# A new order of the side work inside the attention stages, and the second load of the input moved behind the last block of output weights

## The reference

```python
mod = (_silu(c) @ wmod).reshape(1, 6, 1, -1)             # sa, ca, ga, sb, cb, gb
h = _layernorm(x) * (1 + ca) + sa
q = _rmsnorm(h @ wq_a.T, q_ln) @ wq_b.T                  # 32 heads of 64 + 64 (rotary)
ckv, k_pe = split(h @ wkv_a.T); kv = _rmsnorm(ckv, kv_ln) @ wkv_b.T
attn = softmax(causal(q_full @ k_full.T * scale))        # per head, 1024 x 1024
x = x + ga * ((attn @ v) @ wo.T)
h = _layernorm(x) * (1 + cb) + sb
x = x + gb * (down(silu(gate(h)) * up(h)))               # integer weights, width 1376
```

## Time and profile before

| | |
|---|---|
| median of 3 runs | 720.97 us (719.98 to 726.5) |
| the profiled execution, its own time | 720.49 us |
| its span, first to last instruction | 718.7 us |
| PE, DVE, ACT, POOL busy, share of the span | 95%, 73%, 40%, 36% |
| stages 0 to 7 in the trace | 83.81 to about 483 us |
| granted TensorE clock, mean | 0.998 |

### The profile page before, as it was taken

How to read it: one execution, slowest core, us unless ns; L and a number is a source line. 1 busy time by engine, 2 the same in 40 slices (tenths; PEclk the granted TensorE clock), 3 DMA queues, 4 the chain that set the end, 5 groups by cost and what they waited for, 6 DMA issues and landing times.

```text
span 718.7 us, 9328 instructions
## 1 busy us (share of the span) xinstructions
PE 684.4 (95%) x3539; PEld 486.7 (68%) x3539; DVE 526.6 (73%) x762; ACT 288.4 (40%) x427; POOL 258.9 (36%) x164
## 2 busy tenths in 40 slices
PE   2989899999999999999999999899999999999997
PEld 1854477666676675665675665456888888887886
DVE  6878689989999999899899796796882331323432
ACT  4742344534544545445345343352444322322120
POOL 2137622934745645546538204213651000000111
PEclk9999999999999999999999999999999999999999
DMA  8935533303404304313332803810211413100101
GB/s 318 280 90 133 134 77 88 92 17 89 107 1 108 88 8 102 88 41 81 74 81 60 301 2 111 299 59 6 83 29 41 135 46 88 47 1 1 44 31 44
DMA packets 40972, 63.34 MB, mean 88 GB/s; under 512 B 5536, under 2 KB 21664, under 8 KB 39072
## 3 DMA queue, kind: packets, MB, share of 16 engines
q1 hardware_dynamic: 40928, 62.75, 32.0%
HBM read 32.99 MB, written 2.10 MB: 49 GB/s over the span
## 4 chain that ended last, share of the span: by engine, by line
PE 62%; DVE 14%; POOL 8%; DMA 8%; issue 3%; ACT 2%; SPq 2%; DVEq 0%; ACTq 0%; POOLq 0%
PE PS L975 17%; PE PS L992 8%; PE PS L798 7%; DMA Q<-TQ 5%; PE PS L861 5%; PE PS L939 5%; PE PS L868 5%; PE PS L864 5%; PE PS L879 4%; DVE MX L1423 3%; POOL RT L1738 3%; POOL RT L1737 3%; POOL TQ L1776 2%; DVE PR L1518 2%; SPq L562 2%
## 5 line engine op out<-in xcount | busy, mean ns | idle before, releaser
L1423 DVE TRANSPOSE_TENSOR_REDUCE MX<-PS 128x16 f32<-128x512 f32 x288 | 182.5, 686 | 24.3 <-PE PS L798 23.2
L1167 ACT ACTIVATE PR<-PS 128x1024 f32<-128x1024 f32 x108 | 99.5, 929 | 128.7 <-PE PS L868 90.3
L861 PE MATMUL PS<-Q,KH 96*128 96x512 f32 x288 | 118.9, 413 | 4.2 <-ACT PR L1167 2.8
L868 PE MATMUL PS<-Q,KH 97*128 97x512 f32 (+1 forms) x288 | 114.5, 397 | 0.2 <-DMA Q<-NM 0.2
L864 PE MATMUL PS<-Q,KL 96*128 96x512 f32 (+1 forms) x288 | 113.9, 395 | 0.0
L798 PE MATMUL PS<-Q,KH 96*128 96x512 f32 (+1 forms) x288 | 103.4, 422 | 3.9 <-DMA Q<-TQ 2.4
L861 PEld LDWEIGHTS PS<-Q,KH 96*128 96x128 f32 x288 | 54.8, 190 | 40.5 <-ACT PR L1167 16.9
L798 PEld LDWEIGHTS PS<-Q,KH 96*128 96x128 f32 (+1 forms) x288 | 53.0, 191 | 28.1 <-issue 13.4
L1518 DVE TENSOR_TENSOR PR<-PR 128x2048 f32<-128x2048 f32 (+1 forms) x28 | 69.3, 2476 | 0.2
L1645 DVE SCALAR_TENSOR_TENSOR wide<-PS,ffn_s,TQ 128x1024 f32<-128x1024 f32 x10 | 12.8, 1284 | 72.6 <-PE PS L975 72.6
L1167 ACT ACTIVATE wide<-PS 128x1024 f32<-128x1024 f32 (+1 forms) x48 | 45.7, 953 | 50.3 <-PE PS L868 44.2
(11 more groups left out here) (196 smaller groups left out, 1101.3 us busy)
## 6 DMA issues: line engine op xcount, KB each, us to landing
Q<-TQ SPq DMA_DIRECT2D x56, 384.0 KB, 6.5
RT<-in_wo SPq DMA_DIRECT2D x4, 1024.0 KB, 5.5
TQ<-in_wo SPq DMA_DIRECT2D x4, 1024.0 KB, 6.8
Q<-TQ SPq DMA_DIRECT2D x16, 192.0 KB, 3.4
WI<-in_gate_w SPq DMA_DIRECT2D x10, 256.0 KB, 3.3
WI<-in_up_w SPq DMA_DIRECT2D x10, 256.0 KB, 3.9
DI<-in_down_w SPq DMA_DIRECT2D x10, 256.0 KB, 2.7
PR<-in_wmod_c SPq DMA_DIRECT2D x2, 1024.0 KB, 6.3
```

What stands on the lines that cost most here:

```text
L861: pe.matmul(dst, M.KH[0:KR, ks], M.Q[0:KR, w % 2, 0, qb, :, qs], start=True, stop=False)
L868: ins = pe.matmul(dst, M.KH[0:rows, ks], M.Q[0:rows, w % 2, 1, qb, :, qs], start=False, stop=True)
L1167: act.activation(tiles, banks, ACT.Exp).then_inc(S_.p, 1)
L1423: dve.tensor_reduce(M.MX[:, kt, qt // 4, :, qt % 4, :], PS[:, bank_of(turn), :].rearrange("p (h s q) -> p h s q", h=HG, q=L), axis=AX.X, o ...
```

## The change

Two edits. The string list `STAGE` gets another order (stages 0 to 6), and in SP's program the second load of x, with the two waits ahead of it, moves from behind `load_wo(3)` to behind `load_wo(7)`. `LAST` and all functions stay.

```diff
 STAGE = [
-    "w p p", "-v8,9,10,11 p p", "p p -a10", "p", "-a11 p p", "p even0", "", "p p", "p odd0", "p p", "lat0 p low0 a1",
-    "v0,1,2,3 den1 a2 p p", "p", "p p", "p", "p p a3 p", "p", "p p split0", "p p", "p", "p p", "p inv1", "p p",
-    "v4,5 join norm1", "a5", "even1 odd1", "", "a6", "rows a7", "lat1", "", "low1 split1", "v6,7 den0 a8 inv0 norm0",
-    "", "", "a9",
+    "", "", "w p p", "-v8,9,10,11 -a10 p p", "p p", "p -a11 even0 p", "odd0", "p", "p", "p p a1", "v0,1,2,3 den1 p p",
+    "p", "inv1 a2 p p norm1", "", "p", "a3 p p p", "p", "p p", "p p", "v4,5 a5 lat0", "low0 split0 p", "p p", "p p",
+    "p", "p p", "p even1", "p join", "odd1", "a6", "lat1 rows", "", "a7 low1 split1 a8", "v6,7 den0 a9 inv0 norm0",
+    "", "", "",
 ]
@@ sp_program
     for m in range(2, G):
         load_wo(m)
-        if m == 3:
+        if m == G - 1:
             third = max((w, s) for w, s in USES if USES[w, s][0] == 2)
             sp.wait_ge(S_.pv, NSTEP * third[0] + third[1] + 1)
             sp.wait_ge(S_.ad, NADD * third[0] + ADDS.index(third[1]) + 1)
             sp.dma_start(M.x1, t["x"].rearrange("(n p) d -> p n d", p=P)).then_inc(S_.xr, 16)
```

## The result

The changed kernel takes 738.22 us in the median of its runs (732.53 to 739.0), the kernel before, measured beside it, 721.84: a ratio of 1.021, 95% interval 1.018 to 1.0245. It is slower, by 16.4 us (whether by more than 2% the interval leaves open), and the forecast was 721.4, no change. The profiled execution after took 739.0 us, with a span of 737.2.

The account below looks back on a forecast made before the run. PE, busy 95% of the span, was taken to bound the kernel, with a DVE, POOL and ACT chain holding it in the stages. 720.49 + 5.2 - 0.7 - 1.2 - 2.4 gave 721.4 us, range 715.5 to 728.

Parts of the forecast that it names:

- the chain: Stages 1 to 5: `odd1` ends on DVE 42.38 in, then 9.34 to the next stage; 51.8 each, +5.2 us in all.
- The idle time at u35: Near the stage's end PE waits for an exponential: 2.2 us of idle in each of stages 1 to 5.
- Part 10's waits: PE's waits for the queries in stages 1 to 5, about 0.38 us each with restart, were to go.
- The hidden turn: Rival, chance 0.14: DVE ends `odd1` no later than before, stages 1 to 5 stay at 50.76, total 716.2 us.
- the PE bound: Rival, chance 0.05: the next stage no longer hangs on `split1`, waits worth 6.2 us go, total 710.0.
- `a8` did not take the turn before the second sum: Forecast that DVE's addition would not precede POOL's second rotated sum; otherwise 2.28 us longer per stage, 732.8 total.
- the load: x issued behind block 7 lets block 4 of `wo` land earlier: -2.4 us (bounds 0 to -2.4).
- Fold 4: PE's fold of output weights block 4 waited 2.40 us for its transfer; that wait was to go.
- stage 0: 49.15 us against 49.82, -0.7: two more units cover the 1.11 wait for weights, and its clock fall goes too.
- stage 6: PE alone bounds it; two more units cover its wait for the queries: -1.2 us (bounds -0.8 to -1.4).
- the falling clock: Rival, chance 0.11: the clock falls behind PE's 2.2 us idle in five stages, 1.7 us each, 729.9 total.
- the 2.40 wait in stage 7: PE's wait for an output weights block; the clock stayed at 1.00 after it, cited against the clock rival.

Follow-up runs that it names:

- load-alone run: Old stage order, only the second load of x moved behind the last block of output weights, against the kernel before: 717.28 us against 720.87, ratio 0.9952.
- 11 pieces: Old stage order with the load moved, ACT's rounding of the second half in stages 0 to 5 cut into 48-column pieces: 720.24 us.
- the first experiments: The follow-up runs that start with the moved load of x alone in the old stage order: 717.28 us against 720.87 for the kernel before.
- the last kernel: The changed kernel with `odd1` put back right behind `even1`, ahead of the last part and `join`, and `rows` one place later: 710.45 us, ratio 0.985.

## Why the prediction was wrong, and what of it was right

**Right: the chain.** Without falls the kernel takes 721.69, and each step can be found in stage 4 of the kernel with eight matmuls filled in, which starts at 288.58. PE's last matmul of `even1` ends its turn at 326.12, 37.54 in (forecast 37.62). The start of the stage, of the unit behind `even1` and of the next stage on PE, then DVE:

```profile
288.58 0.50 PE L861 MATMUL PS<-Q,KH 96*128 96x512 f32 x1
...
326.12 0.39 PE L861 MATMUL PS<-Q,KH 96*128 96x512 f32 x1
...
340.31 0.50 PE L861 MATMUL PS<-Q,KH 96*128 96x512 f32 x1
```

```profile
326.32 0.69 DVE L1397 TENSOR_TENSOR RT<-PS,cos 128x512 f32<-128x512 f32 x1
...
327.53 0.70 DVE L1427 TRANSPOSE_TENSOR_REDUCE MX<-PS 128x16 f32<-128x512 f32 x1
328.27 1.59 DVE L1438 TENSOR_REDUCE NMj<-MX 128x64 f32<-128x256 f32 x2
329.78 0.67 DVE L1405 TENSOR_TENSOR RT<-PS,sin 128x512 f32<-128x512 f32 x1
...
330.97 2.27 DVE L1522 TENSOR_TENSOR PR<-PR,wide 128x2048 f32<-128x2048 f32 x1
```

`a6` starts 330.97 - 288.58 = 42.39 after the stage (forecast 42.38), and the next stage 9.34 later (9.34). That the first agrees to 0.01 is luck: PE's part came out 0.08 shorter, DVE's start 0.04 earlier, its work 0.13 longer. The idle time at u35 was 2.15 to 2.21 (2.2). Part 10's waits are gone but for one in the first maxima. The hidden turn and the PE bound are refuted with it: `odd1` on DVE follows PE's `even1` and `join`, and `split1` still holds u35. `a8` did not take the turn before the second sum.

**Right: the load.** Fold 4 waits no more, x is issued right behind block 7, and POOL's residual addition, at 514.79, does not wait for it:

```profile
484.88 0.33 SPq L601 DMA_DIRECT2D TQ<-in_wo  x1
485.32 0.39 SPq L672 DMA_DIRECT2D TQ<-in_x  x1
```

**Right, with less behind it: stage 0.** The wait for the weights went, and so did its fall. But the load-alone run waits 1.29 there and shows no fall (stage 0 takes 48.39 instead of 49.82): the 1.70 us of the earlier trace rows were one execution's chance, not a fixed part of the kernel before. Beside an execution without that fall the new order makes stage 0 longer (48.96 against 48.39), not 0.7 shorter.

**Mis-sized: stage 6.** It gained 0.65 (46.62 to 45.97) where 1.2 was reckoned, outside the bounds of 0.8 to 1.4. The wait that went was 0.80, and without it PE can't gain much more than that; and the wait of 0.41 for `join` came instead. That the total still agrees to 0.3 is partly luck: stages 0 to 5 and the load together came out 0.8 shorter than reckoned.

**Wrong: the chance of the falling clock.** The step that failed is the sentence "Against: after the 2.40 wait in stage 7 it stayed at 1.00". One wait without a fall was taken to speak for six waits of nearly the same length, in each execution. The runs show that waits of equal length at one place are followed by a fall in some turns and not in others, and that at u35 of the new order the share rises with the wait: none of 6 at 1.16, 3 of 6 at 1.59, 17 of 18 at 2.15 to 2.21. One draw at 2.40 that came out well says little against that, and stage 0's fall behind 1.11 was a row on the other side. Length alone doesn't decide: at that place in stage 0, behind another wait of 1.44 just ahead of the stage, waits of 0.88 and 1.11 were followed by a fall and waits of 0.73, 0.95 and 1.29 were not. The rival also counted five waits where there are six, since stage 0 has one too. With six in each execution and the shares measured here, some falls were all but sure; the rival belonged at the head, and the range should have held it. The Trainium skill (TensorE: Matmul & The Clock Gate, section "HAM oscillation — how this bites in real kernels") says that a loop which lets TensorE wait on every turn can pay for the slow clock on every turn; these traces agree, with falls at 17 of 18 such waits. The waits in that section's example last some 3 to 5 us; here 2.2 us were enough, and 1.59 in three cases of six.

**Wrong: its price.** The rival put 1.7 on a fall, from stage 0's 3.70 us. The short falls cost that (1.6), but three of the six in the profile after were long, 4.2 us each, and the sixth was not counted. So even the rival, at 729.9, came out 9 us short of the profiled execution.

**What stays open.** Why one wait is followed by a fall and its equal is not, and why a fall begins during the wait or only behind it, with which its length goes (3.3 us, or two or three times that). Also whether the new order is somewhat more prone at 1.6 us: with 2 matmuls filled in all six executions were above 725, with 11 pieces seven of ten lay at or below 720.33. No run had both orders with the same wait and all else equal, and these two ran on different chips.

## What to carry to other kernels

A wait of PE that a reordering makes longer, and that comes back in every turn of a loop, has two prices: its length, and a fall of the clock behind it that may or may not come. One execution's profile of a place where the clock held is little evidence that it will hold: count how many such waits the new kernel has per execution, and put the falls into the sum. Where the wait can't be removed, a few matmuls that nothing reads fill it (here four were enough and two were not); better is to look at what holds it, as here the order of `odd1` and `join` on DVE.

## What the runs showed of the hardware that was not expected

Eight matmuls without use took 16.5 us off the kernel's time, by keeping the clock at 0.999 to 1.000 (738.22 to 721.69).

The nineteen executions of the kernel before beside the first experiments fall into groups by the granted clock: 718.6 to 719.8 us at 1.000, 720.9 to 721.7 at 0.997 and 0.998, 722.4 to 724.0 at 0.995. Nineteen more on another chip are less sharply parted (one took 720.66 at 1.000, one 722.27 at 0.998). The profile that the prediction rests on, 720.49 at 0.998, is one draw of this kind.

A rotated sum takes 3.20 or more on POOL beside an addition on DVE with two inputs from SBUF, and 1.28 or 1.29 beside a reduction (`p` from PSUM, `join` with one input). The Trainium skill (SBUF — State Buffer, section "SBUF: two separate sides") says that a DVE operation with two SBUF inputs holds the shared port pair against POOL for its whole length; the traces agree in both directions. How much of the last kernel's gain comes from moving the sums beside the reductions, and how much from the earlier `odd1`, was not taken apart.
